# Layer norms by pairs of chunks, with 256-column products on tiles of TensorE, in a four-layer network

## The reference

```
def _ln_c(v, eps=1e-06):
    m = jnp.mean(v, axis=1, keepdims=True)
    s = jnp.var(v, axis=1, keepdims=True)
    return (v - m) / jnp.sqrt(s + eps)
...
# one layer (four in all; _ln_t is the same over the last axis, eps 1e-05)
x = x + conv(_ln_c(x), ...)
t = _to_tokens(x)                     # (8, 1024, 64)
t = t + ffn(_ln_t(t), ...)
x = _from_tokens(t, x)
...
# ffn, layers 0 and 3 (16 experts, hidden 128)
logits = jnp.einsum('bsd,de->bse', x, gate_w) + gate_b
top_probs, top_idx = jax.lax.top_k(jax.nn.softmax(logits), 2)   # normalised to sum 1
hidden = jax.nn.silu(h1) * h2
out = sum over experts of (hidden @ w3) * gate
# ffn, layers 1 and 2 (8 experts, hidden 256): gelu(x @ W1 + b1) @ W2 + b2
```

## Time and profile before

| | us |
|---|---|
| median of 3 runs | 2104.28 |
| the profiled execution, its own time | 2102.73 |
| its span on the core | 2100.9 |

### The profile page before, as it was taken

One profiled execution on the slowest core, in us unless ns is written; L12 is line 12 of the kernel. 1 busy time (PEld: TensorE's weight loads), 2 busy tenths in 40 slices (PEclk: granted clock), 3 DMA queues, 4 the chain that ended last, 5 costly groups with the idle time before them and its releaser, 6 DMA issues. The chain is left out here.

```text
span 2100.9 us, 31819 instructions
## 1 busy us (share of the span) xinstructions
PE 1854.2 (88%) x11979; PEld 1077.6 (51%) x11979; DVE 1046.2 (50%) x1331; ACT 1008.4 (48%) x1451; POOL 863.2 (41%) x764
## 2 busy tenths in 40 slices
PE   7686999999697999935799998799999955999998
PEld 3553555554345444422544445576677734555554
DVE  4646666665714222285422223565555535666665
ACT  3333555554114666530466653366666632555554
POOL 0143777774112333340333331312121022777777
PEclk8887999999798999975899998899999987999999
DMA  4002333333001222300022223000000000343333
GB/s 103 1 1 67 108 111 107 110 110 122 0 1 27 81 82 82 88 3 0 22 82 81 78 67 68 1 2 1 1 2 1 2 2 22 108 120 115 113 118 100
DMA packets 71455, 121.29 MB, mean 58 GB/s; under 512 B 16954, under 2 KB 18554, under 8 KB 70658
## 3 DMA queue, kind: packets, MB, share of 16 engines
q1 hardware_dynamic: 71298, 119.20, 19.1%
HBM read 115.48 MB, written 3.67 MB: 57 GB/s over the span
## 5 line engine op out<-in xcount | busy, mean ns | idle before, releaser
L511 POOL TENSOR_TENSOR x<-x,mx_gated 128x512 f32<-128x512 f32 x256 | 328.9, 1285 | 101.9 <-DVE mx_gated L481 101.3
L474 DVE TENSOR_TENSOR mx_hidden<-mx_second,mx_hidden 128x1024 f32<-128x1024 f32 (+1 forms) x256 | 245.3, 958 | 232.8 <-PE mx_second L357 227.8
L610 ACT ACTIVATE mx_hidden<-mx_first,w_bias 128x1024 f32<-128x1024 f32 x256 | 264.1, 1117 | 121.2 <-PE mx_first L357 121.1
L640 POOL TENSOR_TENSOR x<-x,mx_gated 128x512 f32<-128x512 f32 x128 | 164.1, 1282 | 306.6 <-DVE mx_gated L623 306.6
L623 DVE SCALAR_TENSOR_TENSOR mx_gated<-mx_out,w_bias,mx_gates 128x512 f32<-128x512 f32 x128 | 96.2, 751 | 345.0 <-PE mx_out L582 345.0
L462 ACT ACTIVATE mx_hidden<-mx_first 128x1024 f32<-128x1024 f32 x256 | 248.7, 1023 | 13.5
L424 PE MATMUL mx_out<-mx_hidden,w_second 128*64 128x512 f32 x1024 | 248.4, 605 | 2.3 <-issue 2.3
L1520 DVE TENSOR_TENSOR c_near_weights<-c_near_hats 128x768 f32<-128x768 f32 x192 | 177.6, 966 | 133.6 <-PE c_near_turned L1400 133.6
L582 PE MATMUL mx_out<-mx_hidden,w_second 128*64 128x512 f32 x1024 | 233.4, 598 | 0.0
L357 PE MATMUL mx_first<-tokens_high,first_high 64*128 64x512 f32 x1024 | 218.3, 422 | 0.2
L504 POOL TENSOR_TENSOR mx_hidden<-mx_kept,mx_hidden 128x512 f32<-128x512 f32 x128 | 166.4, 1300 | 99.9 <-ACT mx_kept L454 99.9
(11 more groups left out here) (218 smaller groups left out, 2577.5 us busy)
## 6 DMA issues: line engine op xcount, KB each, us to landing
mx_gates<-gate_board SPq DMA_DIRECT2D x768, 128.0 KB, 3.0
w_first<-in_f_first SPq DMA_DIRECT2D x4, 1024.0 KB, 12.2
c_weight<-in_c_weight SPq DMA_DIRECT2D x1, 2304.0 KB
x<-in_x SPq DMA_DIRECT2D x8, 256.0 KB, 4.3
w_second<-in_f_second SPq DMA_DIRECT2D x4, 512.0 KB, 13.1
w_first<-in_f_first SPq DMA_DIRECT2D x4, 512.0 KB, 9.6
out_x<-x SPq DMA_DIRECT2D x16, 128.0 KB, 2.4
gate_board<-xn SPq DMA_DIRECT2D x16, 64.0 KB, 2.5
```

The costliest lines, as they stand in the source:

```text
L474: dve.tensor_tensor(own, second[:, 0:halves, :], own, ALU.mult).then_inc(s.hidden.semaphore, 1)
L511: pool.tensor_tensor(place, place, gated[:, n % GATED, :], ALU.add).then_inc(s.added.semaphore, 1)
L610: act.activation(hidden[:, n % HIDDEN, f], first[:, (n * F + f) % BLOCKS], ACT.Gelu, bias=w.bias1[:, e * F + f:e * F + f + 1]).then_inc(s. ...
L640: pool.tensor_tensor(place, place, gated[:, n % GATED, :], ALU.add).then_inc(s.added.semaphore, 1)
```

## The change

A layer norm now goes by pairs of chunks (four pairs). What was 8 rows becomes the whole height of the array:

- Variances: four products of 256 columns with a 128 x 32 constant (`averages`), each into its own quarter of 32 partitions of `ln_var`. Root and reciprocal are one instruction of 128 x 256 for a pair.
- Spreading: four products of 256 columns from 64 rows each (`spreading`), alternately from the lower and the upper half.
- Centred copies: ScalarE squares both chunks and copies the odd one; VectorE copies the even one.
- Router: the weights are now the stationary operand, four products of 256 columns into quarters; ScalarE copies the result (`ln_kept`), TensorE transposes it back in two pieces, and VectorE adds the bias for that pair at once. `routed` gives the new place of a tile's gates.
- GpSimd makes four of the eight pieces of `first_low`, VectorE the other four.
- ScalarE loads the table for Sqrt at the start of each layer norm, by an instruction on `k.spare`.
- `mean` has four buffers, `var` and `wide` one (of a pair) each. The constant `spreading` has 128 KB, `rows` had 16 KB.

The core of the diff (removed lines of `layer_norm` are left out; they stand above):

```diff
+    PAIRS = CHUNKS // 2
+    COLS = CHUNK // 2
+    QUARTER = P // 4
+    chunks, pairs = turn * CHUNKS, turn * PAIRS
     s, g = k.ln, k.gt
     with ExitStack() as ctx:
         def sb(name, shape):
...
         def ps(name, shape):
             return ctx.enter_context(nc.psum_tensor(f"ln{turn}_{name}", shape, F32))
...
+        square = sb("square", [P, 4, CHUNK])
+        dev = sb("dev", [P, 2, COLS])
+        scale = sb("scale", [P, 2, COLS])
+        mean = ps("mean", [P, 4, CHUNK])
+        var = ps("var", [P, CHUNK])
+        wide = ps("wide", [P, 2, CHUNK])
         if router:
             top_two, w, tokens = router
...
+            raw_pairs = k.mixtures * PAIRS
+            raw = ps("raw", [P, CHUNK])
+            kept = sb("kept", [P, 2, COLS])
+            split_base = k.mixtures * CHUNKS
+            size = w.first.shape[1]
+            pieces = [slice(i * size // CHUNKS, (i + 1) * size // CHUNKS) for i in range(CHUNKS)]
         block = ctx.enter_context(nc.Block())
...
+        def quarter(q):
+            return slice(q * QUARTER, (q + 1) * QUARTER)
...
+        def columns(q):
+            return slice(q % 2 * COLS, (q % 2 + 1) * COLS)
...
         @block.tensor
         def _(pe):
...
+            def means(n):
+                for a in range(2):
+                    i = 2 * n + a
+                    if n >= 2:
+                        pe.wait_ge(s.squared, chunks + i - 3)
+                        pe.wait_ge(s.kept if a else s.centred, pairs + n - 1)
+                    if turn == 0:
+                        pe.wait_ge(k.image_loaded[i * CHUNK // PIX], 16 * HALVES)
+                    pe.matmul(mean[:, i % 4, :], k.centring[:], x[:, chunk(i)],
+                              start=True, stop=True).then_inc(s.mean, 1)
...
+            def variances(n):
+                pe.wait_ge(s.squared, chunks + 2 * n + 2)
+                if n >= 1:
+                    pe.wait_ge(s.dev, pairs + n)
+                for q in range(4):
+                    last = pe.matmul(var[quarter(q), 0:COLS], k.averages[:],
+                                     square[:, (2 * n + q // 2) % 4, columns(q)], start=True, stop=True)
                 last.then_inc(s.var, 1)
...
+            def scales(n):
+                pe.wait_ge(s.scale, pairs + n + 1)
+                if n >= 1:
+                    pe.wait_ge(s.normed, chunks + 2 * n)
+                for q in (0, 2, 1, 3):
+                    last = pe.matmul(wide[:, q // 2, columns(q)], k.spreading[half(q // 2), q % 2, :],
+                                     scale[half(q // 2), n % 2, :], start=True, stop=True)
                 last.then_inc(s.wide, 1)
...
+            def route(n):
+                if n == 0:
                     pe.wait_ge(w.loaded, w.all)
...
+                pe.wait_ge(s.normed, chunks + 2 * n + 2)
+                if n >= 1:
+                    pe.wait_ge(g.raw_kept, raw_pairs + n)
+                    pe.wait_ge(g.logits, raw_pairs + n)
+                for q in range(4):
+                    at = (2 * n + q // 2) * CHUNK + q % 2 * COLS
+                    last = pe.matmul(raw[quarter(q), 0:COLS], w.router[:], xn[:, at:at + COLS], start=True, stop=True)
+                last.then_inc(g.raw, 1)
...
+            def turns(n):
+                pe.wait_ge(g.raw_kept, raw_pairs + n + 1)
+                for c in range(COLS // P):
+                    last = pe.transpose(raw[:, COLS + c * P:COLS + (c + 1) * P],
+                                        kept[:, n % 2, c * P:(c + 1) * P], k.identity[:])
+                last.then_inc(g.turned, 1)
...
             if turn == 0:
                 pe.wait_ge(k.constants, k.constants_all)
...
+            if router:
+                staggered((0, means), (4, turns), (1, variances), (2, scales), (3, route))
+            else:
+                staggered((0, means), (1, variances), (2, scales))
             if turn == 0:
                 pe.wait_ge(k.more_constants, 16 * 2)
...
         @block.scalar
         def _(act):
...
+            def squares(n):
+                for a in range(2):
+                    i = 2 * n + a
+                    act.wait_ge(s.mean, chunks + i + 1)
+                    if n >= 2:
+                        act.wait_ge(s.var, pairs + n - 1)
+                    act.activation(square[:, i % 4, :], mean[:, i % 4, :], ACT.Square).then_inc(s.squared, 1)
+                i = 2 * n + 1
+                act.copy(xn[:, chunk(i)], mean[:, i % 4, :]).then_inc(s.kept, 1)
...
+            def deviations(n):
+                act.wait_ge(s.var, pairs + n + 1)
+                if n >= 2:
+                    act.wait_ge(s.scale, pairs + n - 1)
+                act.activation(dev[:, n % 2, :], var[:, 0:COLS], ACT.Sqrt, bias=k.eps[eps][:]).then_inc(s.dev, 1)
...
+            def highs(n):
+                for i in (2 * n, 2 * n + 1):
+                    act.wait_ge(s.normed, chunks + i + 1)
+                    act.copy(tokens[0][:, chunk(i)], xn[:, chunk(i)]).then_inc(g.high, 1)
...
+            def keep(n):
+                act.wait_ge(g.raw, raw_pairs + n + 1)
+                if n >= 2:
+                    act.wait_ge(g.turned, raw_pairs + n - 1)
+                act.copy(kept[:, n % 2, :], raw[:, 0:COLS]).then_inc(g.raw_kept, 1)
...
+            act.activation(k.spare[:, 0:1], k.eps[eps][:], ACT.Sqrt)
+            if router:
+                staggered((0, squares), (1, deviations), (3, highs), (3, keep))
+            else:
+                staggered((0, squares), (1, deviations))
...
         if router:
             @block.gpsimd
             def _(pool):
...
                 pool.wait_ge(w.loaded, w.all)
...
+                for i in range(CHUNKS):
                     pool.tensor_copy(w.high[:, pieces[i]], w.first[:, pieces[i]]).then_inc(g.w_high, 1)
...
+                for i in range(CHUNKS):
+                    if i < CHUNKS // 2:
+                        pool.wait_ge(g.w_high, split_base + i + 1)
+                        pool.tensor_tensor(w.low[:, pieces[i]], w.first[:, pieces[i]],
+                                           w.high[:, pieces[i]].bitcast(F32), ALU.subtract)
+                    pool.wait_ge(g.high, split_base + i + 1)
+                    pool.tensor_tensor(tokens[1][:, chunk(i)], xn[:, chunk(i)],
+                                       tokens[0][:, chunk(i)].bitcast(F32), ALU.subtract)
...
         @block.vector
         def _(dve):
...
+            def centres(n):
+                i = 2 * n
+                dve.wait_ge(s.squared, chunks + i + 1)
+                dve.tensor_copy(xn[:, chunk(i)], mean[:, i % 4, :]).then_inc(s.centred, 1)
...
+            def split(n):
+                i = CHUNKS // 2 + n
+                dve.wait_ge(g.w_high, split_base + i + 1)
+                dve.tensor_tensor(w.low[:, pieces[i]], w.first[:, pieces[i]],
+                                  w.high[:, pieces[i]].bitcast(F32), ALU.subtract)
...
+            def scales(n):
+                dve.wait_ge(s.dev, pairs + n + 1)
+                if n >= 2:
+                    dve.wait_ge(s.wide, pairs + n - 1)
+                dve.reciprocal(scale[:, n % 2, :], dev[:, n % 2, :]).then_inc(s.scale, 1)
...
+            def norm(n):
+                dve.wait_ge(s.centred, pairs + n + 1)
+                dve.wait_ge(s.kept, pairs + n + 1)
+                dve.wait_ge(s.wide, pairs + n + 1)
+                for a in range(2):
+                    own = xn[:, chunk(2 * n + a)]
+                    dve.tensor_tensor(own, own, wide[:, a, :], ALU.mult).then_inc(s.normed, 1)
...
+            def logits(n):
+                E, own = top_two.experts, slice(n * 4 * CHUNK_TILES, (n + 1) * 4 * CHUNK_TILES)
+                if n == 0:
+                    dve.wait_ge(w.loaded, w.all)
+                dve.wait_ge(g.turned, raw_pairs + n + 1)
+                turned = raw[:, COLS:CHUNK].rearrange("p (t e) -> p t e", e=SWIGLU.experts)[:, :, 0:E]
+                dve.tensor_tensor(top_two.logits[:, own, :], turned, spread(w.router_bias[:], 1, 4 * CHUNK_TILES),
+                                  ALU.add).then_inc(g.logits, 1)
...
+            def statistics(n):
+                for i in (2 * n, 2 * n + 1):
+                    dve.wait_ge(s.normed, chunks + i + 1)
+                    ins = dve.bn_stats(stats[:, i, :], xn[:, chunk(i)])
+                    if i == CHUNKS - 1:
+                        ins.then_inc(k.bn.stats, 1)
...
             if router:
...
+                staggered((0, centres), (0, split), (4, logits), (1, scales), (2, norm))
             elif stats:
...
+                staggered((0, centres), (1, scales), (2, norm), (2, statistics))
                 dve.wait_ge(k.bn.stats, 1)
             else:
...
+                staggered((0, centres), (1, scales), (2, norm))
...
+def routed(i, q):
+    return (i // 2 * 2 + q % 2) * 4 + i % 2 * 2 + q // 2
...
     def turn(self, pe, i, turned):
         for q in range(CHUNK_TILES):
             last = pe.transpose(turned[0:HALVES * self.E, q * P:(q + 1) * P],
...
```

(32 more changed lines are left out.)

105 lines of the change are left out of this document (11 added, 94 removed).

## The result

The changed kernel takes 2037.01 us (median of 4 runs, 2035.74 to 2038.15) against 2104.16 us for the kernel before on the same chip: a ratio of 0.9681 (95% interval 0.9665 to 0.9698), 67.1 us less. The profiled execution took 2036.29 us, its span is 2034.4 us, the mean granted clock 0.923 (0.926 before). The forecast was 2051: the direction held, and 14 us of the gain were missed. The measured time lies 1 us inside the fast end of the stated range, 2036 to 2073, and outside the case that had got 0.60 of the chance, 44 to 60 us saved.

What follows compares the result with a forecast made beforehand. TensorE was taken to bound the eight layer norms. Savings of 64.5 us at full clock and 46 with a clock fall average 55, less 2 is 53; 2102.7 less 53 is 2049.7, plus 1.5 gives 2051, range 2036 to 2073.

Steps and rivals of the forecast that it cites:

- TensorE bounds the norms before: Eight old layer norms, 262.8 us together: TensorE busy nearly throughout, 34.70 of 37.15 us in the second.
- Products on tiles: Norms' tiled products: four quarters at once, a pair's variances 0.45 us, spreading 0.86, plus 0.12 at each change between groups.
- The tiles run one after another: Rival on the norms' tiled products: no overlap, TensorE bounds again, only some 4 us saved, 2100; chance 0.03.
- each of their eight weight loads costs as now: Rival: quarters overlap, but variances and router take 0.9 us each and the clock falls; 31 saved, 2073; chance 0.17.
- The reciprocal doesn't shrink: VectorE's reciprocal in every norm: 1.72 us a pair instead of 1.88.
- VectorE bounds plain norms: Plain norms: VectorE is the bound from 5.6 us on; 21.8, 21.8 and 22.5 us for third, fifth and seventh.
- GpSimd bounds the norms of 16 experts: Router norms of 16 experts: GpSimd starts tokens_low near 12.2 us, needs 13.9, and ends at 26.1, after VectorE's 24.8.
- The clock: New norms: a fall to half clock at 14 us costs 6.1 us in those without a router, 12.5 in the four with.
- the two sums: Total saving over the eight norms: 64.5 us at full clock, 46 if the clock falls; their mean is 55.
- the fourth rival: Rival for all norms: the clock never falls and all waits are as counted; 64.5 us saved, 2040; chance 0.16.
- The 2 us taken off for unseen waits: Total saving: 2 us subtracted from the mean of 55 for waits not seen, giving 53.
- The full-clock sum: All eight norms at full clock: 19.4 + 3.7 + 41.4 = 64.5 us saved.

Runs made afterwards that it cites:

- x4: The changed kernel with each pair's four variance products 128 columns wide, accumulating one after another into the whole of ln_var: 2053.15 us, ratio 0.9753.
- x9: The changed kernel with a pair's variances as eight products of 128 columns, root and reciprocal 128 x 128, output complete: 2031.86 us, ratio 0.9659.
- x3: The changed kernel with the reciprocal on 128 of a pair's 256 columns, the others 1.0: 3628.54 us on altered data, only the norms can be read.
- x7: The changed kernel with three more centring products, result unused, ahead of the last two spreadings of each plain norm: 2035.22 us, ratio 0.9677.
- x2: The changed kernel with GpSimd's four pieces of first_low moved ahead of its first wait for tokens_high: 2031.47 us, ratio 0.9648.
- x1: The changed kernel with GpSimd making all eight pieces of first_low again and VectorE none: 2051.74 us, ratio 0.9747.

## Why the prediction was off by 14 us, point by point

- **TensorE bounds the norms before**: right. Its busy time there fell from 248.9 us (the eight of the earlier trace rows) to 145.6, and the norms by 64.7. The signs that the prediction named for this came: the windows sum to 199.8, between its 195 and 220, and what lies outside them moved by 1.8 in all.
- **Products on tiles**: right. Variances 0.57 to 0.64 a pair (forecast 0.45 + 0.12), spreading 1.13 (0.86 + 0.12), and x4 shows the overlap. "The tiles run one after another" and "each of their eight weight loads costs as now" fell; x9 doubled the loads at no cost.
- **The reciprocal doesn't shrink**: right, 1.74 to 1.75 against 1.72.
- **VectorE bounds plain norms**: right for the kernel as it is, since VectorE has hardly any idle time between its first reciprocal and the last spreading, but TensorE and ScalarE are close behind: with 3.2 us less of reciprocal 1.3 arrive (x3, x9), and with 5.0 more of variances 2.7 do (x4). The saving was 3.4, 4.7, 5.4 and 7.7 against 3.7, 6.5, 6.5 and 6.4 at full clock: 21.2 against 23.1. The 7.7 are luck: I had counted 2.3 for a begin of the seventh norm at half clock, and it began at full. In the third VectorE needed 15.7 us from its first reciprocal on, where I had 14.2: 0.95 of the difference is the last spreading at half clock, some 0.3 the durations.
- **GpSimd bounds the norms of 16 experts**: right to 0.2 us. For 8 experts I let VectorE's 24.8 bound; at full clock it ended at 22.59, and GpSimd at 24.04 (forecast 24.4). VectorE's tail chain was 2.7 us, not 3.2, and it waited less than I took. The router norms saved 11.0, 11.3, 11.3 and 9.8, together 43.5 against 41.4.
- **The clock**: the step that failed. "If it falls at 14 us ... 12.5 less over the four" and 6.1 in the others. In the second and fourth norm the clock was 1.00 until TensorE's last product, so the doubling of the chain spreading, router, transpose never came; in plain norms only the last spreading was hit, for 0.95 us. So the price of one spreading at half clock was about right (0.86 forecast), the number of products that the fall would reach was not. Of 18.6 us forecast some 4 came, four times 0.95. I had drawn the fall from the old norm's tail, and from TensorE's idle share after. But the new tail is idler than the old one and keeps the clock. My 53 lay between the two sums; the fourth rival, "clock never falls", which had 0.16 of the chance, was nearly the truth in the norms that carry two thirds of the gain. The 2 us taken off for unseen waits had no row behind them.
- The full-clock sum, 64.5, agrees with the 64.7 of the windows, partly by luck: plain norms 1.9 too high, routers 2.1 too low, and both lengths of the first norm 2 us short.
- **Sums that don't hold**: the price of the serial rival. Its own 27.5 and 35.5 us, against the earlier trace rows, give some 11 us saved, 2093, not 4 and 2100. And 128 KB at 154 GB/s are 0.8 us, not 0.5. The first doesn't enter the 2051, the second by 0.3 us.

What stays open: why the clock holds in the new tails at 5.80 busy of 9.62 us, and fell in the old one at 5.14 of 6.70. x7 shows that centring products keep it up, and x4 that longer variance products do so in three plain norms; which property of the products does it was not separated. Nor was it settled why one plain norm begins at half clock and another at full clock (the third and the seventh of the same execution, and the seventh again at half clock in x2, x3 and x9), which moves a norm by 1.7 to 3.1 us and made x7's total uncertain. The two lengths of the first convolution are open too.

## What to carry to other kernels

When TensorE stops being the bound, walk each of the other engines in its own program order from its first wait: GpSimd's idle 5.70 us ahead of independent work cost 1.2 to 3.0 us in each norm with a router, and moving four instructions gave 5.5 us. Small products on quarter or half tiles are cheap enough to trade for shorter elementwise work: eight products of 128 columns instead of four of 256 cost nothing, and nearly halved the reciprocal. But a shorter step gives back only what the next chain leaves: 1.3 of 3.2 us here. Don't price a drop of the clock from one stretch of the old kernel: bound it from both sides, and let the case without it keep more than a sixth of the chance. And before stretches of two executions are compared, look at the clock at which each begins.

## What the runs showed of the hardware that I had not expected

- VectorE and GpSimd slow each other when both subtract or cast weights: the same `first_low` on VectorE took 1.06 us beside GpSimd's casts and 0.67 alone, GpSimd's 1.71 beside VectorE and 1.27 alone, and its eight casts 4.97 us against 4.53 before. With no weight pieces on VectorE (x1) the casts are back at 4.5 and GpSimd's first piece at 1.28.
- A reciprocal costs by its columns, not its rows: 1.75 us for 128 x 256, 0.95 for 128 x 128, 0.94 for 8 x 128 and 0.55 for 128 x 64.
- TensorE kept its full clock while busy 5.80 of 9.62 us in short products on tiles, and products of 128 columns were as fast, column by column, as those of 256 (0.64 and 1.16 us in x9 against 0.64 and 1.13).
